# Graph attention with preceding layer norm: one node table with a dump row per edge, and the segment limits of the last two pairs summed on TensorE

## What is computed

```python
h = relu(layernorm(x))
xs, xd = h @ W_src.T, h @ W_dst.T            # per node, 8 heads of 32
alpha = leaky(sum(xs[src]*att_src[type]) + sum(xd[dst]*att_dst[type]))   # edges and self loops
a = exp(alpha - segment_max(alpha, dst)); a = a / segment_sum(a, dst)
out = segment_sum(xs[src] * a * edge_weight, dst) + bias
g = layernorm(out + h); y = layernorm(g + ffn(g)); result = x + y
```

## Time and profile before

| | us |
|---|---|
| median of three runs | 3086.09 |
| lowest, highest | 3082.42, 3091.74 |
| profiled execution | 3095.26 |
| its span | 3093.4 |
| its mean granted TensorE clock | 0.964 of full speed |

### The profile page before, as it was taken

How to read it: one execution, slowest core, us unless ns; L and a number is a source line. 1 busy time by engine, 2 the same in 40 slices (tenths; PEclk the granted TensorE clock), 3 DMA queues, 4 the chain that set the end, 5 groups by cost and what they waited for, 6 DMA issues and landing times.

```text
span 3093.4 us, 55233 instructions
## 1 busy us (share of the span) xinstructions
PE 2827.9 (91%) x18391; PEld 2572.6 (83%) x18391; DVE 2308.6 (75%) x6031; ACT 1801.0 (58%) x3180; POOL 2203.0 (71%) x1683
## 2 busy tenths in 40 slices
PE   4666646699999999999999999999999999999998
PEld 3666535489999999999999999999999999999998
DVE  4665575577777777777777777777777777777776
ACT  3555434456666666666666666666666666666664
POOL 5555555477777777777777777777777777777773
PEclk9788877899999999999999999999999999999999
DMA  6454455555555555555555555555555555555551
GB/s 141 99 101 102 99 126 174 157 134 144 147 146 144 144 144 146 148 147 146 145 148 150 149 147 144 144 146 148 144 148 144 145 144 145 145 148 148 146 138 63
DMA packets 597311, 430.65 MB, mean 139 GB/s; under 512 B 430515, under 2 KB 534075, under 8 KB 597028
## 3 DMA queue, kind: packets, MB, share of 16 engines
q1 hardware_dynamic: 563698, 347.95, 38.9%
q0 software_dynamic: 31312, 77.03, 14.1%
q10 hardware_dynamic: 2018, 2.13, 0.2%
HBM read 247.76 MB, written 179.26 MB: 138 GB/s over the span
## 4 chain that ended last, share of the span: by engine, by line
PE 86%; DVE 4%; ACT 3%; another core or an unknown queue 3%; issue 3%; POOL 1%; DMA 0%; ACTq 0%; DVEq 0%; SPq 0%; POOLq 0%
PE ps_f L1459 35%; PE ps_x L1498 9%; PE ps_a L1474 6%; PE ps_a L1476 6%; PE ps_t L1474 6%; PE ps_t L1476 6%; PE ps_a L1475 6%; PE ps_t L1475 6%; PE ps_x L457 2%; ACT h L415 2%; PE ps_a L1442 1%; PE ps_t L424 1%; PE ps_a L457 1%; DVE zt_lo L440 1%
## 5 line engine op out<-in xcount | busy, mean ns | idle before, releaser
L837 ACT ACTIVATE act_hi<-ps_f,hidden_bias 128x512 fp32r<-128x512 f32 x784 | 537.1, 685 | 924.1 <-PE ps_f L1459 923.7
L1319 DVE TENSOR_TENSOR act_lo<-ps_f,act_hi 128x512 fp32r<-128x512 f32 x784 | 539.7, 688 | 461.5 <-ACT ps_f L838 390.1
L1459 PE MATMUL ps_f<-zt_hi,ffn_hi 128*128 128x512 f32 x1568 | 617.5, 394 | 2.5 <-DVE zt_lo L1277 1.6
L1459 PE MATMUL ps_f<-zt_hi,ffn_lo 128*128 128x512 f32 x1568 | 619.4, 395 | 0.0
L1459 PE MATMUL ps_f<-zt_lo,ffn_hi 128*128 128x512 f32 x1568 | 617.1, 394 | 0.0
L838 ACT ACTIVATE ps_f<-ps_f,hidden_bias 128x512 f32<-128x512 f32 x784 | 510.1, 651 | 0.0
L683 POOL DMA_INDIRECT arena<-sums,node_rows x391 | 403.9, 1033 | 121.5 <-issue 102.9
L1474 PE MATMUL ps_a<-ffn_hi,act_hi 128*128 128x256 f32 x1568 | 439.8, 280 | 0.0
L1476 PE MATMUL ps_a<-ffn_hi,act_lo 128*128 128x256 f32 x1568 | 439.1, 280 | 0.0
L1475 PE MATMUL ps_a<-ffn_lo,act_hi 128*128 128x256 f32 x1568 | 437.9, 279 | 0.0
L1474 PE MATMUL ps_t<-ffn_hi,act_hi 128*128 128x256 f32 x1560 | 437.6, 281 | 0.0
(11 more groups left out here) (229 smaller groups left out, 6753.9 us busy)
## 6 DMA issues: line engine op xcount, KB each, us to landing
xb<-in_x SPq DMA_DIRECT2D x97, 512.0 KB, 5.0
z_rows<-arena SPq DMA_DIRECT2D x97, 512.0 KB
arena<-z_rows SPq DMA_DIRECT2D x388, 128.0 KB
out<-arena SPq DMA_DIRECT2D x97, 512.0 KB, 4.4
h_rows<-h SPq DMA_DIRECT2D x96, 512.0 KB
arena<-h_rows SPq DMA_DIRECT2D x384, 128.0 KB
msgs<-arena SPq DMA_DIRECT2D x49, 256.0 KB
arena<-msgs SPq DMA_DIRECT2D x49, 256.0 KB
```

The source lines that it names most:

```text
L837: act.activation(act_hi[:, m % AB, :], ps_f[:, m % 2, :], ACT.Gelu, bias=hidden_bias[:, m:m + 1]).then_inc(act_hi_ready, 1)
L1319: dve.tensor_tensor(act_lo[:, m % AB, :], ps_f[:, m % 2, :], act_hi[:, m % AB, :].bitcast(F32), ALU.subtract).then_inc(act_lo_ready, 1)
L1459: ins = pe.matmul(ps_f[:, m % 2, 0:cols], ffn1[a][:, k, m * P:(m + 1) * P], zt[b][:, i.par, k, 0:cols], start=(j == 0), stop=(j == 3 * KC ...
```

## The change

The four tables become one. It has a dump row for every edge (12,544 in place of 128), so no two edges write the same word, `place` waits for nothing, one table is cleared, one is read back, and the minima go. The dump row's number is now a tensor (`gin`, edge number plus NROWS) in place of a scalar per partition. `ends_cleared`, `ends_at` and four matmuls make the limits of pairs 47 and 48 without DMAs of the records: `ends_at` holds, for each of the last four chunks, row 0 = the chunk's unit row of `ident` and row 127 = its row of `up`, so that a matmul with it adds the chunk's first and last sums where they belong. Its eight small rows are copied by SyncE at pair 20, behind the masks. Pairs 45 and 46 are copied as before. SyncE waits for `fix_pe` before it goes on to the node groups.

```diff
-    row_of = [nc.dram_tensor(f"row_of_{i}", (NROWS + P, 1), ...) for i in range(RB)]
+    row_of = nc.dram_tensor("row_of", (NROWS + EP, 1), I32, kind="Internal").ap()
-            for i in range(RB):
-                sp.dma_start(row_of[i][0:NR, :]..., node_rows[:, :]).then_inc(rows_cleared, 16)
+            sp.dma_start(row_of[0:NR, :]..., node_rows[:, :]).then_inc(rows_cleared, 16)
+                if j.n == 20:                                   # SP, in pair
+                    sp.wait_ge(masks_made, 1)
+                    for i in range(2 * ENDS_PE):
+                        c = NCH - 2 * ENDS_PE + i
+                        sp.dma_start(ends_at[0:1, i, :], ident[c:c + 1, 0:NCH]).then_inc(ends_made, 16)
+                        sp.dma_start(ends_at[P - 1:P, i, :], up[c:c + 1, :]).then_inc(ends_made, 16)
-                if j.n >= NPAIR - ENDS_KEPT:                    # SP, in sum_pair
+                if NPAIR - ENDS_KEPT <= j.n < NPAIR - ENDS_PE:
+                    sp.wait_ge(ends_cleared, 2)
             steps(sp, sum_pair, 1 - SB, NPAIR, *SUM_LOOP)
+            sp.wait_ge(fix_pe, 1)
-                b = c.off % RB                                  # POOL, in place
-                wait_count(pool, rows_stored[b], 16 * c.before(RB))
-                pool.indirect_dma_start(row_of[b], ...).then_inc(rows_stored[b], 16)
+                pool.indirect_dma_start(row_of, ...).then_inc(rows_stored, 16)
-            pool.wait_ge(node_rows_set, RB - 1)
+            pool.wait_ge(node_rows_in, 16)
+            act.wait_ge(ends_cleared, 2)                        # ahead of load_ends
-            for i in range(RB):
-                act.wait_ge(rows_stored[i], 16 * ((NCH + RB - 1 - i) // RB))
-            for to, of in zip([node_rows[:, :]] + [other_rows...], row_of):
-                act.dma_start(to, of[0:NR, :]...).then_inc(node_rows_in, 16)
+            act.wait_ge(rows_stored, 16 * NCH)
+            act.dma_start(node_rows[:, :], row_of[0:NR, :]...).then_inc(node_rows_in, 16)
-            link(dve.tensor_copy(trash, flag_i), flag_sum, 1)
-            link(dve.tensor_scalar(target_f, dst_f[:, 1:NCH + 1], trash, None, ALU.subtract), target_step, 5)
+            link(dve.tensor_scalar(gin, target_i, float(NROWS), None, ALU.add), target_step, 5)
+            link(dve.tensor_tensor(target_f, dst_f[:, 1:NCH + 1], gin, ALU.subtract), target_step, 6)
+                dve.memset(ends_at[:, :, :], 0.0).then_inc(ends_cleared, 1)          # pair 10
+                    dve.memset(fix_ends[P // 2:NCH], 0.0).then_inc(ends_cleared, 1)  # sum pair 2
-            dve.wait_ge(fix_in, 16 * (2 + 2 * ENDS_KEPT))
+            dve.wait_ge(fix_in, 16 * (2 + 2 * (ENDS_KEPT - ENDS_PE)))
-            dve.wait_ge(node_rows_in, 16 * RB)
-            for i in range(RB - 1):
-                link(dve.tensor_tensor(node_rows[:, :], node_rows[:, :], other_rows[:, i, :], ALU.min), ...)
+            pe.wait_ge(ends_made, 16 * 4 * ENDS_PE)
+            for k in range(ENDS_PE):
+                j = NPAIR - ENDS_PE + k
+                pe.wait_ge(rec_made, j + 1)
+                for q in range(2):
+                    pe.matmul(ps_t[0:NCH, 0, 0:D], ends_at[:, 2 * k + q, :], rec_out[:, 2 * (j % RO) + q, :], ...)
             pe.wait_ge(fix_step, 1)
-            pe.matmul(ps_a[0:NCH, 0, 0:D], up[0:NCH, :], fix_ends[0:NCH, 1, :], start=True, stop=True)
+            pe.matmul(ps_t[0:NCH, 0, 0:D], up[0:NCH, :], fix_ends[0:NCH, 1, :], start=False, stop=True)
```

More of the change, by code:

```diff
@@ L90 @@
 XB = 4
-RB = 4
 MB = 4
@@ L96 @@
 ENDS_KEPT = 4
+ENDS_PE = 2
 SPLITS = 9
@@ L140, in build @@
     sums = nc.dram_tensor("sums", (EP + NCH + P, D), F32, kind="Internal").ap()
-    row_of = [nc.dram_tensor(f"row_of_{i}", (NROWS + P, 1), I32, kind="Internal").ap() for i in range(RB)]
+    row_of = nc.dram_tensor("row_of", (NROWS + EP, 1), I32, kind="Internal").ap()
     msgs = nc.dram_tensor("msgs", (EP, D), F32, kind="Internal").ap()
@@ L177, in build @@
         zt = [sb(f"zt_{n}", [P, 2, KC, GR], F32R) for n in ("hi", "lo")]
+        with nc.sbuf_tensor("ends_at", [P, 2 * ENDS_PE, NCH], F32) as ends_at:
+            pass
         act_hi = sb("act_hi", [P, AB, GR], F32R)
@@ L220, in build @@
         target_i, place_i = records[:, :, 0], records[:, :, 1]
-        trash, flag_f = part([1]), part([1])
+        flag_f = part([1])
         flag_i = part([1], I32)
@@ L312, in build @@
          scan_step ends_ready ends_turned carry_ready carry_turned diff_ready exp_ready sums_ready sums_carried coef_ready coef_turned coef_out
-         vals_ready line_turned distance_made eq_ready agg_done rec_made fix_in fix_step fix_pe fix_made fix_stored target_ready place_ready target_step node_rows_set
+         vals_ready line_turned distance_made eq_ready agg_done rec_made ends_cleared ends_made fix_in fix_step fix_pe fix_made fix_stored target_ready place_ready target_step node_rows_set
          sp_gate pool_gate dve_gate node_rows_in
@@ L326, in build @@
         x_in = [sem(f"x_in_{i}") for i in range(NB)]
-        rows_stored = [sem(f"rows_stored_{i}") for i in range(RB)]
+        rows_stored = sem("rows_stored")
         gathered = [sem(f"gathered_{i}") for i in range(XB)]
@@ L674, in _ @@
             steps(pool, pair, 0, NPAIR, *PAIR_LOOP)
-            steps(pool, place, len(PLACE_AT), NCH, NCH, NCH, RB)
+            steps(pool, place, len(PLACE_AT), NCH, NCH, NCH, 4)
             def gather_records(g):
@@ L899, in _ @@
                 act.wait_ge(agg_stored[k % RO], 16 * (k // RO + 1))
+            act.wait_ge(ends_cleared, 2)
             for c in range(2):
                 load_ends(act, c)
-            for i in range(RB):
-                act.wait_ge(rows_stored[i], 16 * ((NCH + RB - 1 - i) // RB))
-            for to, of in zip([node_rows[:, :]] + [other_rows[:, i, :] for i in range(RB - 1)], row_of):
-                act.dma_start(to, of[0:NR, :].rearrange("(p t) o -> p (t o)", p=P)).then_inc(node_rows_in, 16)
+            act.wait_ge(rows_stored, 16 * NCH)
+            act.dma_start(node_rows[:, :], row_of[0:NR, :].rearrange("(p t) o -> p (t o)", p=P)).then_inc(node_rows_in, 16)
             act.wait_ge(fix_made, 1)
@@ L991, in _ @@
             link(dve.tensor_scalar(minus_dst, dst_f[:, 1:NCH + 1], -1.0, None, ALU.mult), target_step, 4)
-            link(dve.tensor_scalar(target_f, dst_f[:, 1:NCH + 1], trash, None, ALU.subtract), target_step, 5)
-            link(dve.tensor_tensor(target_f, target_f, last, ALU.mult), target_step, 6)
-            dve.tensor_scalar(target_i, target_f, trash, None, ALU.add).then_inc(target_ready, 1)
+            link(dve.tensor_scalar(gin, target_i, float(NROWS), None, ALU.add), target_step, 5)
+            link(dve.tensor_tensor(target_f, dst_f[:, 1:NCH + 1], gin, ALU.subtract), target_step, 6)
+            link(dve.tensor_tensor(target_f, target_f, last, ALU.mult), target_step, 7)
+            dve.tensor_tensor(target_i, target_f, gin, ALU.add).then_inc(target_ready, 1)
             def message(j):
@@ L1376, in _ @@
         def _(pe):
-            pe.wait_ge(consts, 12)
-            pe.wait_ge(flag_sum, 3)
+            pe.wait_ge(consts, 11)
+            pe.wait_ge(flag_sum, 2)
             pe.matmul(ps_a[0:1, 0, 0:1], flag_f, ones[:, :], start=True, stop=True).then_inc(flag_pe, 1)
@@ L1530, in _ @@
             steps(pe, sum_pair, -1, NPAIR, *SUM_LOOP)
+            pe.wait_ge(ends_made, 16 * 4 * ENDS_PE)
+            pe.wait_ge(nt_lo, 2 * KC)
+            for k in range(ENDS_PE):
+                j = NPAIR - ENDS_PE + k
+                pe.wait_ge(rec_made, j + 1)
+                for q in range(2):
+                    pe.matmul(ps_t[0:NCH, 0, 0:D], ends_at[:, 2 * k + q, :], rec_out[:, 2 * (j % RO) + q, :], start=(k == 0 and q == 0), stop=False)
             pe.wait_ge(fix_step, 1)
-            pe.wait_ge(rec_made, NPAIR)
-            pe.matmul(ps_a[0:NCH, 0, 0:D], up[0:NCH, :], fix_ends[0:NCH, 1, :], start=True, stop=True).then_inc(fix_pe, 1)
+            pe.matmul(ps_t[0:NCH, 0, 0:D], up[0:NCH, :], fix_ends[0:NCH, 1, :], start=False, stop=True).then_inc(fix_pe, 1)
             steps(pe, nodes, -1, NG + 1, *NODE_LOOP)
```

27 lines of the change are left out of this document (13 added, 14 removed).

## The result

The changed kernel took 3115.97 us (median; 3111.23 to 3120.43) beside 3086.38 us for the kernel before (median of six runs, the three known ahead of the prediction among them): a ratio of 1.0094, interval 1.0066 to 1.0121. Forecast were 3078.1 us and a range up to 3090. It is slower by 29.6 us, and no case of the prediction with a price near that had more than a chance of 0.08.

A forecast was written before the change was run, and what follows sets the result against it. TensorE was taken to bound the node loop from about 600 us, so gains ahead count fully. Passage 3.0, scatters 4.2 and start 0.8 sum to 8.0 us: 3086.1 - 8.0 = 3078.1 us, range 3068 to 3090.

The forecast's parts named there:

- What bounds the kernel: TensorE bounds the node loop from about 600 us, which the change leaves alone; each microsecond won ahead counts one for one.
- The scatters: Scatters on POOL beside the sums: without waits the first burst overlaps the sums 9.3 us less, gaining 4.2 us (0 to 9.3).
- The first (the stall ends with the burst): Rival: the sums' stall ends with the first scatter burst, so all 9.3 us come back: 3073.0 us; chance 0.24.
- the second (not the scatters'): Rival: the stall beside the sums is not the scatters', only passage and start count: 3082.3 us; chance 0.24.
- The fourth: Rival: one table is slower, scatters into one small region drain more slowly than issued, steps above 1.56 us: 3103 us; chance 0.08.
- The passage: From last record to first lift sum: limits by TensorE instead of late DMA copies gain 3.0 us, between 0 and 6.
- the third rival: Passage gains 0: load_ends' reads land as late as the old copies and first gathers slow behind moved h reads; 3081.1 us, chance 0.08.
- The start: Kernel's start: three of four table clears go, freeing DMA time ahead of TensorE's first transposes; 0.8 us gain, between -0.3 and 3.
- At nothing: Costed at zero: two VectorE memsets of about 0.4 us each and eight SyncE copies, 4.7 us in all, taken as covered.

The follow-up runs named there:

- clean session: Session on a chip where the kernel before took 2968 to 2971 us; of twelve traces one shows a wait with a remote releaser, of 1.2 us.
- late one: Session where the kernel before took 3086 to 3095 us and every trace shows long waits with a remote releaser in the first 600 us.
- the two kernels with a tighter or later burst: Changed kernel, one table: at most two scatters in flight, 1.0160; four in flight with 14 first-stage scatters moved behind that stage, 1.0061; both beside the kernel before at 2968 to 2971.

## Why the prediction was wrong

**What bounds the kernel** held: from the first gather to the end it is 2508.4 and 2508.6 us, and in all nineteen traces between 2507.3 and 2512.7, so that what was won or lost ahead of it counted one for one.

**The scatters** are the step that failed, in its sign. The prediction read the crawl of the sums beside the first burst as a cost of the time in which burst and sums overlap, took 4.2 us for 9.3 us less of it, and set the ends at 0 and 9.3. Its first half came true: the burst ended 11.2 us earlier and the sums' first stretch sped up as said. What it missed is that the removed waits did a second thing, which the reason given for them (two chunks on one dump row) doesn't mention: they kept the number of scatters in flight at four or fewer. Without that, late counts stand in the scans (+17.6 us, for which the sum had no term) and beside the second burst, against the first stretch's gain: +4.2 us for the sums as a whole, where it had -4.2 for both together. The claim "25 scatters cost nothing there" held for spaced scatters only. The rows that should have given a bound below nothing were in the prediction: 52.3 us of remote waits in a stage with a single scatter every third pair could be completions that come late beside scatters, and nothing excluded that denser scatters bring more. (The run without scatters bears that out in part: it keeps 23.9 us of those waits.) An unknown releaser was costed as if its only dependence was overlap; its bounds had to be open on both sides.

**The rivals.** The first (the stall ends with the burst) and the second (not the scatters') both fail: without scatters 53 us go, with denser ones 30 come. The fourth had the side right and the mechanism wrong: it asked for steps above 1.56 us, and the step was 1.26; four tables without waits lose as much (1.0069). The Trainium skill's rule ("DMA: Bandwidth & Descriptors", Specifications) of read-modify-write under 512 B spoke for it. No cost of it shows here: one table is 0.9996 to four tables' 1.0000 in a clean session, with waits in both, and 1.0006 in a late one.

**The passage** was forecast at 3.0 us, between 0 and 6. Up to the gather it gave 1.7 instead of 3.6: load_ends' reads landed at 599.66, 2.5 us from the end of issue (597.19; forecast 2.2), the matmuls were covered, but L1544 still took 0.91 us and the store of the limits 3.03 instead of 1.74, since SyncE's wait now lets the h store go at the same moment. Then the first group's landing took 7.08 us instead of 5.24. From the last record to the first lift sum it is 20.5 us against 20.4 before; in the clean session 19.5 against 18.0. The gain is gone: the third rival's second half, to which I had given 0.08 together with a first half that did not come. The lower end for the landing, -2, was the right size; taking only 0.6 of it was the mistake.

**The start** came as forecast and did not last. ScalarE's first L790 starts at 42.7 instead of 43.7, and at 35.4 instead of 36.7 in the clean session; the first stage as a whole ends no earlier (425.8 against 425.3, 320.8 against 318.8).

**At nothing:** the prediction said that nobody waits for the layer-norm step at place 33. Not so: ScalarE waited 9.6 us for it ahead of L812, and the two kernels with a tighter or later burst showed what that costs when it comes later. For this change the step came earlier and VectorE's idle time ahead of its second scans stayed at 2.0 us, so the sum was not touched.

**The range and the session.** The forecast of 8 us less is not seen in either kind of session: 29.6 us more in the late one, 2968.4 against 2968.5 in the clean one. Small slips in the working change nothing of this: the lower end of 3068 is explained by the first rival with a passage of 6, which gives 3070.0, and 497.4 less 9.3 us is 488.1, not 487.

**What stays open:** what makes a count arrive late, in whose way the scatters are, and why three of seven sessions have it. The trace names no releaser. The record numbers the chips, and number 1 ran a late session and, some 16 minutes later, a clean one; if the number means the same chip both times, the kind belongs to the moment and not to the chip. That the removed waits are the loss is shown by taking them out with one table and with four, and by putting them back with one. Whether they help by the number in flight or by the longer step (1.56 us against 1.26) is not shown: no kernel spaced its scatters without waiting for a landing. Why the kernel before crawled beside its first burst and not beside its second, at nearly the same step, is open too, and so is whether two in flight would be better still in a late session. None of the kernels beat the kernel before by more than 0.1% in any session and kept the result whole.

## What to carry to other kernels

A wait can do more than what it was written for: before one is removed, ask what it spaces, and price the denser stream on everything that runs beside it, the other engines' own semaphore counts included. Where a profile shows waits without a releaser, a change to the traffic beside them has no bounded price, on either side; run it in several sessions, since a result from one kind (1.009 late, 1.000 clean) doesn't hold in the other. And a small step placed in a paced queue is late with it: look who waits for it before the pacing is tightened.

## What the runs showed of the hardware

Not expected: the same kernel differs by 118 us (2968 and 3086) between sessions. Of the 129.8 us between the two profiled spans 106.5 lie in the first stage (318.8 and 425.3) and almost none behind the first gather (2508.0 and 2508.4). VectorE waited up to 8.3 us for the counts of operations of its own that had ended, and where the counts' records are complete (the changed kernel's reciprocal) they stand 0.7 or 1.4 us apart for operations 0.26 us apart. And scatters of 128 words, which cost a clean session 7.5 us for 98 of them, with four in flight as without any wait (two in flight cost 46 us more there, with GpSimd waiting 97.4 us in 40 places for their landings), cost a late one about 53 us spaced (3086.1 - 3032.6) and some 82 unspaced (3114.7 - 3032.6).
